# POOL takes the value products, the gating and the row sum of an RWKV recurrence from VectorE

## The reference, cut to what matters

```python
k, v, r = (mixed @ W for each of att_Wk, att_Wv, att_Wr)
def step(carry, kv_t):                      # over the 256 tokens
    out = (e1 * aa + e2 * vv) / (e1 * bb + e2)
    return ((e1b * aa + e2b * vv, e1b * bb + e2b, p2), out)
rwkv = sigmoid(r) * out
x = x + rwkv @ att_Wo
...
return x + sigmoid(xr2 @ ffn_Wr) * (square(relu(xk2 @ ffn_Wk)) @ ffn_Wv)
```

## Time and profile before

| what | value |
|---|---|
| median of 3 runs | 1112.25 us (1111.33 to 1115.49) |
| the profiled execution: its time | 1110.54 us |
| its span (first to last instruction) | 1108.8 us |
| mean granted TensorE clock | 0.884 |
| busy over the span | PE 863.4, DVE 749.3, ACT 643.2, POOL 531.5 us |
| RWKV block, 603.9 to 843.9 us: busy of 240.0 | DVE 211.67, ACT 163.95, PE 154.20, POOL 71.38 us |

### The profile page before, as it was taken

One profiled execution on the slowest core, in us unless ns is written; L12 is line 12 of the kernel. 1 busy time (PEld: TensorE's weight loads), 2 busy tenths in 40 slices (PEclk: granted clock), 3 DMA queues, 4 the chain that ended last, 5 costly groups with the idle time before them and its releaser, 6 DMA issues. The chain is left out here.

```text
span 1108.8 us, 19595 instructions
## 1 busy us (share of the span) xinstructions
PE 863.4 (78%) x5834; PEld 697.3 (63%) x5836; DVE 749.3 (68%) x2380; ACT 643.2 (58%) x1342; POOL 531.5 (48%) x673
## 2 busy tenths in 40 slices
PE   2887676665569989998995647777748998999993
PEld 2642554554458868997995223444536898999991
DVE  5658778999888477212668599999889734223734
ACT  4253887777755324664664656677676663555551
POOL 0000555767427777775773777000001565777650
PEclk9999677888859999998998768789986898999997
DMA  7999000000071116656774111000005343334214
GB/s 195 290 183 71 0 1 0 1 0 0 2 269 53 50 52 198 198 162 179 202 188 121 48 44 47 6 1 1 1 0 165 134 126 81 82 93 146 79 39 154
DMA packets 146757, 101.44 MB, mean 91 GB/s; under 512 B 22256, under 2 KB 138352, under 8 KB 145648
## 3 DMA queue, kind: packets, MB, share of 16 engines
q1 hardware_dynamic: 133872, 74.10, 26.7%
q0 software_dynamic: 12800, 26.31, 8.1%
HBM read 45.69 MB, written 50.48 MB: 87 GB/s over the span
## 5 line engine op out<-in xcount | busy, mean ns | idle before, releaser
L1295 POOL DMA_INDIRECT e_xs<-h_tok,rows_of x128 | 126.5, 988 | 58.2 <-issue 36.2
L805 ACT ACTIVATE mask<-ps_q,k_neg 128x256 bf16<-128x256 f32 x256 | 101.0, 489 | 30.6 <-PE ps_q L946 30.6
L946 PE MATMUL ps_q<-q_parts,pick 128*128 (+1 forms) x256 | 57.5, 358 | 54.7 <-DVE mask L679 40.9
L1338 POOL DMA_INDIRECT e_ys_tok<-e_y_rows,e_out_ids x80 | 79.4, 993 | 38.8 <-ACT e_y_rows L1687 22.3
L1474 PE MATMUL e_ps_gu<-e_w_all,e_x_turned 128*128 x384 | 93.1, 386 | 0.4 <-ACT e_x_turned L1654 0.4
L2039 DVE TENSOR_TENSOR e_hidden<-e_ps_gu,e_hidden 128x512 f32<-128x512 f32 x48 | 33.2, 691 | 87.6 <-ACT e_hidden L1660 87.3
L2059 DVE COPY e_w_here<-e_w_all 128x512 f32 x80 | 34.9, 438 | 82.6 <-PE e_ps_up L1506 81.3
L2586 POOL DMA_INDIRECT c_got<-e_ys,rows_of x64 | 71.4, 1115 | 34.1 <-issue 19.2
L1295 POOL DMA_INDIRECT e_xs<-e_h_ids,e_rows_of x64 | 62.6, 978 | 51.3 <-DVEq L1873 32.4
L1506 PE MATMUL e_ps_up<-e_x_turned,e_w_here 128*128 128x128 f32 x640 | 86.3, 279 | 0.8 <-ACT e_x_turned L1654 0.8
L946 PEld LDWEIGHTS ps_q<-q_parts,pick 128*128 128x128 f32 x256 | 43.5, 238 | 61.8 <-issue 40.4
(11 more groups left out here) (448 smaller groups left out, 2470.4 us busy)
## 6 DMA issues: line engine op xcount, KB each, us to landing
e_xs<-zeros SPq DMA_DIRECT2D x2, 6144.0 KB, 34.6
e_x_rows<-e_xs SPq DMA_DIRECT2D x48, 256.0 KB
e_ys<-e_y_rows SPq DMA_DIRECT2D x48, 256.0 KB, 2.5
e_w_all<-in_w SPq DMA_DIRECT2D x4, 1536.0 KB, 12.6
e_x_rows<-e_xs SPq DMA_DIRECT2D x20, 260.0 KB
e_xs<-zeros SPq DMA_DIRECT2D x2, 2560.0 KB, 42.6
e_h_ids<-h_tok SPq DMA_DIRECT2D x16, 256.0 KB, 3.6
e_w_all<-in_w SPq DMA_DIRECT2D x4, 1024.0 KB
```

The lines of the kernel that those rows point to most:

```text
L805: last = nc.scalar.activation(mask[u][QS // 2 + j][keys][:, h * T:(h + 1) * T], psq[1][:, h * T:(h + 1) * T], ACT.Sign, bias=k_neg[u][:, k ...
L946: last = nc.tensor.matmul(psq[0 if on_dve else 1][:, h * T:(h + 1) * T], pick[:, (quad * HQ + h) * P:(quad * HQ + h + 1) * P], q_parts[:, ...
L1295: nc.gpsimd.indirect_dma_start(out=xs[part], out_offset=bass.IndirectOffsetOnAxis(ap=rows_of[:, j:j + 1], axis=0), in_=rows, in_offset=Non ...
L1338: nc.gpsimd.indirect_dma_start(out=ys_tok, out_offset=bass.IndirectOffsetOnAxis(ap=out_ids[:, i:i + 1], axis=0), in_=tile(y_rows[q % YB], ...
```

## The change

For groups 3 to 7 (GA = 3) POOL makes the two products with v into two new tiles, `add_term` and `put_term` (`value_terms`), and multiplies the finished numerator with the gate as r * num, then + num (`gated_sums`). For groups 2 to 7 (GR = 2) POOL makes the output rows in two steps, `prod *= 0.5` in place and the sum with `h_tok` (`rows_out_sum`). DVE waits for POOL at four places: before the scans into `a_st`, before the numerator's last sum, before `wkv`, and before the rows' statistics. Every other instruction stays as it is.

```diff
-                    co.mark(nc.vector.tensor_tensor(add, add, v, ALU.mult))
-                    yield
+                    if g < GA:
+                        co.mark(nc.vector.tensor_tensor(add, add, v, ALU.mult))
+                        yield
...
+                    if g >= GA:
+                        dve.wait_ge(terms_made, FROM + 2 * (g - GA) + 1)
                     for i in range(BPG):
                         cols = slice(i * T, (i + 1) * T)
                         co.mark(nc.vector.tensor_tensor_scan(a_st[:, i * W1T + 1:(i + 1) * W1T], carry[:, cols],
-                                                             add[:, cols], 0.0, ALU.mult, ALU.add))
+                                                             (add if g < GA else add_term)[:, cols], 0.0, ALU.mult,
+                                                             ALU.add))
...
-                    co.mark(nc.vector.tensor_tensor(num[:, :], num[:, :], put, ALU.add))
+                    if g < GA:
+                        co.mark(nc.vector.tensor_tensor(num[:, :], num[:, :], put, ALU.add))
+                    else:
+                        dve.wait_ge(terms_made, FROM + 2 * (g - GA) + 2)
+                        nc.vector.tensor_tensor(num[:, :], num[:, :], put_term[:, :], ALU.add).then_inc(num_made, 1)
...
+                    else:
+                        dve.wait_ge(num_gated, FROM + g - GA + 1)
                     nc.vector.scalar_tensor_tensor(wkv[g % 2][:, :], num[:, :], 0.5, den[:, :], ALU.mult,
...
+                def value_terms(g):
+                    e, v = ex[g % 2], kvr["v"][g % 2][:, :]
+                    pool.wait_ge(exped, FROM + g + 1)
+                    pool.wait_ge(kvr_sb, FROM + 3 * g + 2)
+                    pool.wait_ge(num_made, FROM + g - GA)
+                    nc.gpsimd.tensor_tensor(add_term[:, :], e[:, 2 * GW:3 * GW], v, ALU.mult).then_inc(terms_made, 1)
+                    nc.gpsimd.tensor_tensor(put_term[:, :], e[:, GW:2 * GW], v, ALU.mult).then_inc(terms_made, 1)
+
+                def gated_sums(g):
+                    pool.wait_ge(kvr_sb, FROM + 3 * g + 3)
+                    pool.wait_ge(num_made, FROM + g - GA + 1)
+                    nc.gpsimd.tensor_tensor(add_term[:, :], num[:, :], kvr["r"][g % 2][:, :], ALU.mult).then_inc(gate_made, 1)
+                    pool.wait_ge(gate_made, FROM + g - GA + 1)
+                    nc.gpsimd.tensor_tensor(num[:, :], num[:, :], add_term[:, :], ALU.add).then_inc(num_gated, 1)
+
+                def rows_out_sum(g):
+                    pool.wait_ge(prod_ready, FROM + g + 1)
+                    pool.wait_ge(o_sb, FROM + g + 1)
+                    nc.gpsimd.tensor_scalar(prod[:, :], prod[:, :], 0.5, None, ALU.mult).then_inc(prod_halved, 1)
+                    pool.wait_ge(prod_halved, FROM + g - GR + 1)
+                    nc.gpsimd.tensor_tensor(group(y_tok, g), prod[:, :], group(h_tok, g), ALU.add).then_inc(y_out, 1)
+
+                for n in range(GA + 1, GROUPS + 3):
+                    if n - 1 < GROUPS:
+                        value_terms(n - 1)
+                        gated_sums(n - 1)
+                    if n - 3 >= GR:
+                        rows_out_sum(n - 3)
                 env["renew_semaphores"](pool)
```

More of the change, by code:

```diff
@@ L2194, in rwkv @@
         front_rows = sem("front_rows")
+        terms_made, num_made, num_gated = map(sem, ("terms_made", "num_made", "num_gated"))
+        GA, GR = 3, 2
+        gate_made, prod_halved = map(sem, ("gate_made", "prod_halved"))
+        add_term, put_term = tb("add_term", GW), tb("put_term", GW)
         scale_y1, shift_y1, shift_x1, x_rstd = (env[n] for n in ("scale_y1", "shift_y1", "shift_x1", "rstd"))
@@ L2310, in output_sums @@
                     yield
-                    co.mark(nc.vector.tensor_tensor(put, put, v, ALU.mult))
-                    yield
+                    if g < GA:
+                        co.mark(nc.vector.tensor_tensor(put, put, v, ALU.mult))
+                        yield
                     co.wait()
-                    co.mark(nc.vector.tensor_tensor(num[:, :], num[:, :], put, ALU.add))
+                    if g < GA:
+                        co.mark(nc.vector.tensor_tensor(num[:, :], num[:, :], put, ALU.add))
+                    else:
+                        dve.wait_ge(terms_made, FROM + 2 * (g - GA) + 2)
+                        nc.vector.tensor_tensor(num[:, :], num[:, :], put_term[:, :], ALU.add).then_inc(num_made, 1)
                     yield
@@ L2319, in output_ratio @@
                     co.wait()
-                    co.link(nc.vector.scalar_tensor_tensor(num[:, :], kvr["r"][g % 2][:, :], 1.0, num[:, :], ALU.add, ALU.mult))
+                    if g < GA:
+                        co.link(nc.vector.scalar_tensor_tensor(num[:, :], kvr["r"][g % 2][:, :], 1.0, num[:, :], ALU.add,
+                                                               ALU.mult))
+                    else:
+                        dve.wait_ge(num_gated, FROM + g - GA + 1)
                     nc.vector.scalar_tensor_tensor(wkv[g % 2][:, :], num[:, :], 0.5, den[:, :], ALU.mult,
@@ L2344, in rows_out @@
                 def rows_out(g):
[L2345 to L2348, removed]
+                    if g < GR:
+                        dve.wait_ge(prod_ready, FROM + g + 1)
+                        nc.vector.scalar_tensor_tensor(group(y_tok, g), prod[:, :], 0.5, group(h_tok, g), ALU.mult,
+                                                       ALU.add).then_inc(y_out, 1)
+                        yield
                     dve.wait_ge(y_out, FROM + g + 1)
```

## The result

The changed kernel takes 1130.34 us (median of 4 runs, 1129.9 to 1135.79) where the kernel before takes 1111.79 beside it: a ratio of 1.0183 (95% interval 1.0163 to 1.0203), +20.3 us. (The two medians lie 18.6 us apart; the ratio, of runs made beside each other, is what is used from here on.) The forecast was 1133. The profiled execution took 1130.44 with a span of 1128.7, granted clock 0.874: +19.9 on the execution that the sum was made against.

A forecast was written before the change was run, and what follows sets the result against it. DVE's sums up to `wkv` were taken to bound the loop, PE close behind. Holds +11.3, iteration 9 +1.8 and block's end +8.0 gave +21.1 on 1110.54, 1131.6; with 1.71 to the median, 1133 us, range 1118 to 1141.

The forecast's parts named there:

- POOL holds DVE's two-tensor operations: In the loop, each POOL operation meeting DVE's scans or two-tensor operations holds them about 1.15 us; +2.27 a group, +11.3 for five.
- Rival 2: No hold between long operations in the loop: -4.5 there, tail stays at +8.0, so +3.5, 1116 us; chance 0.14.
- PE lets at most 0.9 a group through: In the loop, PE was only 0.89 us idle when `wkv` came, so a group cannot gain more than about 0.9 us.
- The size of the hold: DVE held 2.30 at the value products, 0.74 and 1.15 at the mixes: 4.19 us a group, less 1.92 of work lost.
- 2 x 1.15: POOL's two value products each hold DVE's scans and two-tensor operations up to the numerator's end by 1.15: 2.30 us a group.
- Iteration 9, +1.8: No reciprocal covers group 6's halving and row sum; they meet front sums and `f_mix` for group 7: 2 x 0.9 us.
- The halving, 0.8: POOL's multiplication of the output rows by 0.5 was taken as 0.8 us, nearer a 128x512 cast's 0.61 than 1.81.
- rival 3: POOL waits in turn for DVE; halving and row sum slide off the reciprocal's cover: 7.2 us more, 1140; chance 0.07.
- The block's end, +8.0: POOL's 61 clears and 61 increments, 9.0 us, run exposed behind group 7's halving; next layer starts at 851.9, +8.0 us.
- rival 1: At the block's end POOL's sequencer renews semaphores beforehand, hidden: +1.5 in place of +8.0, 1127 us; chance 0.12.
- The sum: Loop +11.3, iteration 9 +1.8 and block's end +8.0 make +21.1 us on the profiled execution's 1110.54.

The follow-up runs named there:

- the hold taken away: POOL writes zeros in place of both value products of groups 3 to 7 and gates under the reciprocal, against the kernel before: 1106.94 us, ratio 0.9950.
- The zeros: POOL's value products of groups 3 to 7 replaced by writing zeros, gating under the reciprocal, against the kernel before: 1106.94 us, ratio 0.9950.

## Why the prediction came out right, and where its terms failed

- **POOL holds DVE's two-tensor operations** (the step that decided): right. Scans, products and mixes beside POOL's two-tensor operations grew, `product` and the reciprocal did not, and each part by itself holds its own victims. Rival 2 is out: it needed a hold below 1.4 us a group, and it was 3.5 in group 5. What the rival would have given came out near (-5.6 measured with the hold taken away, -4.5 forecast), but not by its step: that PE lets at most 0.9 a group through was read from group 4, and the traces show up to 2.0 in groups 3, 6 and 7 and nothing in group 4.
- **The size of the hold:** 3.5 in group 5 where 4.19 was forecast. The mixes were nearly exact (0.70 and 1.00 against 0.74 and 1.15); the value products held 1.84 and not 2.30. By the rows POOL's second product (1.65 in place of 1.28) waited for the scan that ran, and the operation behind it lost only what was left. The "2 x 1.15" took the price of two separate meetings for two operations in a row. Groups 3, 4 and 6 met other operations, some of them short (gathered rows, steps of a root, a row sum), and were held 3.9, 2.8 and 4.4 by the same reading, the 4.4 with 0.35 of a halving.
- **Iteration 9, +1.8:** wrong. There the halving and the sum of group 6 lay beside DVE's sums of the front rows and their statistics from 834.0 to 837.2, and none grew: the sums took 0.69 and 0.68. Behind it is the step that gave every POOL operation the same hold; the halving, beside both sums, held them by nothing, and POOL's own sum lay beside the statistics, which read one tensor. Loop and iteration 9 together were forecast at +13.1 and came to +7.3 to +8.8 in the traces, +5.7 (3.8 to 7.4) in the times.
- **The halving, 0.8:** mis-sized. It took 1.49 alone and 1.92 beside a mix; the cast was the wrong neighbour, four times the small operation (1.81) the better one. It cost nothing for groups 2, 3, 5 and 6; for group 4 it met the second mix at 798.02 and held it to 1.10, 0.35 more; in the tail it cost 0.7. The row sums fell under the reciprocal for groups 2 to 5 (rival 3 is out).
- **The block's end, +8.0:** the mechanism was right and a term was missing. The clears stood behind the waiting POOL instructions (rival 1 is out) and took their 9.0; the drain that ends the block was not counted. Its row was there to be read in the kernel before: 14.6 us from 685.6, hidden, ended 5.3 after the last gather. I listed what the change moves to the end, and not what the end itself does on that engine. +14.0 in the trace, 14.7 by the ratios.
- **The sum:** +21.1 forecast, +20.3 measured. That it fits to 1 us is luck: an overestimate of 4 to 7 us in the loop met an underestimate of 6 at the end. The direction, the two places and what waits there were right; the sizes were not.

By the Trainium skill (SBUF — State Buffer, 🔬 SBUF: two separate sides) a VectorE operation with two SBUF inputs contends only with a GpSimd one that reads SBUF, and whichever starts first has the port pair for its whole instruction. The zeros, which read nothing and held no scan, agree. The halving does not: it was under way from 742.86, and the mix that came at 743.35 ended at 744.45, before POOL at 744.79; it lost 0.35 and not POOL's remaining 1.4. The measurement decides.

## What to carry to other kernels

In this loop moving elementwise work from DVE to POOL can pay only where DVE meanwhile runs something that POOL doesn't hold, here a reciprocal; put there, the same two operations held nothing (-0.7, within the noise), and put one step earlier they cost more than they saved (+2.3). Before work is moved to the end of an engine's block, read what that end already does while hidden (semaphore renewals, a drain behind gathers), because the last engine to arrive exposes all of it; both can be moved ahead of the wait. Relief on one engine of a tight loop must be followed into the others, group by group: where PE comes after `wkv` anyway, an earlier `wkv` brings nothing.

## What the runs showed of the hardware

- The first drain of POOL's queue behind indirect gathers ended 5.3 us after the last instruction ahead of it (a gather, a row sum, an increment), and this is paid once: after an early drain the next one took 1.38, all of it the wait for a running sum. In the attention, without gathers, a drain ended 0.1 after POOL's last sum.
- POOL's multiplication of a 128x512 tensor by a constant takes 1.49 us, longer than its product of two tensors (1.27), and held a DVE operation on two tensors by at most 0.4, in iteration 9 by nothing. Writing zeros takes 0.52 and holds nothing.
- Two executions of one kernel differed by 1.5 us in this loop, as TensorE was or was not at its lower level behind the same wait of 3.48 us (granted clock 0.59 and 1.00 from 760 to 764 us); a single trace of a loop of 210 us is good to about that.

Left open: why the traces put the loop's price (7.3 to 8.8) somewhat above the times (5.7, at most 7.4), and how much of the loss was TensorE's clock and not the hold (0.84 from 740 to 790 us in the changed kernel, 0.90 and 0.86 in the two traces of before); the value products could not be placed under a reciprocal, since their exponentials come only when DVE's sums begin.
